# Expert block: 125-row transfers in two parts, the output bias ahead of the tiles, two gathers added in the next block, context roots moved

## What is computed

```python
# layer 0
q = _ln(latents, ...);  x = latents + _mha(q, q, ...)              # L0_sa
qc = _ln(x, ...);       kv = _ln(tokens, ...)
x = x + _mha(qc, kv, ...)                                          # L0_ca
h = _ln(x, ...);        logits = h @ rw.T + rb                     # L0_moe: 8 experts, 2 for each token
vals, idx = jax.lax.top_k(logits, K);  gates = softmax(vals)
h1 = gelu(einsum('nd,efd->enf', hf, fc1_w) + fc1_b[:, None, :])
eo = einsum('enf,edf->end', h1, fc2_w) + fc2_b[:, None, :]
x = x + (eo[idx_f, arange(N)[:, None], :] * gates_f[..., None]).sum(axis=1)
# layer 1
x = features + _mha(xn, xn, xn, ..., causal)                       # L1_sa
x = x + _mlp(_ln(x, ...), ...)                                     # L1_m1
x = x + _mha(_ln(x, ...), encoder_output, encoder_output, ...)     # L1_ca: keys and values of the raw context
x = x + _mlp(_ln(x, ...), ...)                                     # L1_m2
# layers 2 and 3: L2_ca, L2_m1, L2_sa, L2_m2, L3_ca, L3_m
```

## Time and profile before

| | us |
|---|---|
| median of 3 runs | 2048.26 |
| lowest, highest | 2045.43, 2050.31 |
| the profiled execution | 2057.58 |
| its span | 2055.8 |
| TensorE busy, weight loads busy | 1776.4, 1237.2 |
| DVE, ACT, POOL busy | 1332.9, 866.2, 629.1 |

### The profile page before, as it was taken

The page is one execution under the profiler, slowest core; times in us unless marked ns, Lnnn a source line. Parts: engine busy times, 40 slices in busy tenths (PEclk is TensorE's granted clock), DMA queues, the critical chain, the costliest instruction groups (busy, mean ns, idle before and its releaser), DMA issues.

```text
span 2055.8 us, 34270 instructions
## 1 busy us (share of the span) xinstructions
PE 1776.4 (86%) x10630; PEld 1237.2 (60%) x10630; DVE 1332.9 (65%) x3354; ACT 866.2 (42%) x2513; POOL 629.1 (31%) x732
## 2 busy tenths in 40 slices
PE   5969999769996878988779999896888979898988
PEld 4746665558985656655565555483444845455567
DVE  5866767301117876788666676796677966556665
ACT  3735554322334643565324444342332435444521
POOL 2325555210022234676320000130000325455534
PEclk9979998879998978999789999997998989999999
DMA  4100000468862000002100010101000100000200
GB/s 167 37 20 15 13 7 16 147 217 301 307 236 82 0 1 31 32 30 71 67 8 16 16 69 0 42 11 62 0 0 19 55 1 12 23 11 11 72 1 18
DMA packets 36627, 115.15 MB, mean 56 GB/s; under 512 B 2961, under 2 KB 23345, under 8 KB 29345
## 3 DMA queue, kind: packets, MB, share of 16 engines
q1 hardware_dynamic: 33968, 107.33, 15.2%
q0 software_dynamic: 2544, 6.43, 1.0%
HBM read 99.34 MB, written 14.40 MB: 55 GB/s over the span
## 4 chain that ended last, share of the span: by engine, by line
PE 44%; issue 20%; DVE 14%; POOL 14%; ACT 4%; DMA 3%; SPq 1%; POOLq 0%; DVEq 0%; ACTq 0%
POOL arena L2020 11%; PE ps L1008 7%; PE ps L1048 4%; PE ps L821 4%; PE ps L873 3%; PE ps L1168 3%; PE ps L1152 3%; PE ps L927 3%; PE ps L816 3%; PE ps L947 2%; PE ps L891 1%; PE ps L863 1%; DMA wml<-in_wm_L_moe 1%; PE ps L933 1%; ACT arena L1286 1%
## 5 line engine op out<-in xcount | busy, mean ns | idle before, releaser
L2020 POOL TENSOR_TENSOR arena<-arena,rinv 112x375 f32<-112x375 f32 (+1 forms) x448 | 371.1, 830 | 489.9 <-DVE rinv L1675 479.7
L891 PEld LDWEIGHTS ps<-cst,arena 112*125 112x125 f32 (+1 forms) x1408 | 188.1, 184 | 176.6 <-POOL arena L2020 88.9
L891 PE MATMUL ps<-cst,arena 112*125 112x112 f32 (+1 forms) x1408 | 247.0, 294 | 45.2 <-POOL arena L2020 39.9
L1286 ACT ACTIVATE arena<-ps,negmax 112x375 f32<-112x375 f32 (+1 forms) x384 | 190.6, 501 | 168.2 <-DVE negmax L1670 167.8
L1684 DVE COPY arena<-ps 125x336 f32<-125x336 f32 x384 | 190.8, 497 | 47.3 <-PE ps L891 44.9
L2073 POOL TENSOR_TENSOR w_split_sb<-wml,w_split_sb 128x512 fp32r<-128x512 f32 (+1 forms) x40 | 45.9, 1148 | 527.0 <-ACT w_split_sb L1352 525.1
L1670 DVE TENSOR_REDUCE negmax<-ps 112x1 f32<-112x375 f32 (+1 forms) x288 | 158.3, 550 | 70.9 <-PE ps L863 61.9
L1008 PE MATMUL ps<-h_split_sb,w_split_sb 128*128 128x448 f32 x768 | 179.7, 383 | 17.8 <-DVE h_split_sb L1559 7.1
L1286 ACT ACTIVATE arena<-arena,negmax 112x112 f32<-112x112 f32 (+1 forms) x256 | 125.4, 491 | 139.1 <-DVE negmax L1659 97.0
L1008 PEld LDWEIGHTS ps<-h_split_sb,w_split_sb 128*128 128x128 f32 x768 | 150.4, 198 | 35.9 <-DVE h_split_sb L1559 13.2
L816 PE MATMUL ps<-wat,arena 128*125 128x256 f32 (+1 forms) x608 | 153.5, 390 | 16.8 <-DVE arena L1600 9.5
(11 more groups left out here) (221 smaller groups left out, 3186.7 us busy)
## 6 DMA issues: line engine op xcount, KB each, us to landing
wml<-in_wm_L_moe SPq DMA_DIRECT2D x21, 1028.0 KB, 7.7
wml<-in_wm_L_moe SPq DMA_DIRECT2D x21, 1024.0 KB, 7.7
craw<-in_ctx SPq DMA_DIRECT2D x40, 375.0 KB
wml<-in_wm_L_m SPq DMA_DIRECT2D x3, 3072.0 KB, 13.8
wat<-in_wa_L_ca SPq DMA_DIRECT2D x2, 2560.0 KB, 10.2
wml<-in_wm_L_m SPq DMA_DIRECT2D x2, 2048.0 KB, 10.1
keys_hbm<-arena SPq DMA_DIRECT2D x8, 375.0 KB
values_hbm<-vz SPq DMA_DIRECT2D x8, 375.0 KB
```

Source lines behind the costliest of these rows:

```text
L891: last = nc.tensor.transpose(ps[0:blk.kp, T_BANK + s % blk.t_banks, o:o + S], buf[:, i * blk.nk + q * blk.kp:i * blk.nk + (q + 1) * blk.kp ...
L1286: last = go(probs[0:S, s % blk.nprobs, i * nk:(i + 1) * nk], src[:, i * nk:(i + 1) * nk], ACT.Exp, scale=-1.0 if blk.mask == "input" else ...
L2020: pool.tensor_tensor(p3, p3, r3, ALU.mult).then_inc(scaled, 1)
```

## The change

Five edits.

1. In the expert block each 125-row transfer (context loads, value stores) is issued as two: rows 0 to 111 and rows 112 to 124 (`transfer`). The semaphore counts follow (32 for each load, 48 for each pair of stores).
2. The output bias: the eight small matmuls stand together behind context 4 and ahead of tile 0, into banks 1 to 4; DVE adds all eight there, and TensorE waits for the eight adds before the up part of tile 0.
3. DVE adds the gathered rows of batches 0 to 5 at the end of the expert block and those of batches 6 and 7 at the end of batch 0 of L1_sa, with a second run of the 13 statistics operations for these two. `gate` gets a place of its own.
4. The context statistics of L0_sa: the means and variances (6 operations) and the roots for L0_ca (12) go into the drain of L0_sa, the roots for L3_ca (13) behind the last tile of the expert block.
5. `out_banks`: behind a dense feed-forward block batch 7 goes to bank 5, if the next block doesn't use bank 5 for its pieces (L1_m1, L2_m2 and L3_m).

```diff
+            def transfer(dst, src, signal):
+                for r in (slice(0, KP // 16 * 16), slice(KP // 16 * 16, KP)):
+                    sp.dma_start(dst[r], src[r]).then_inc(signal, 16)
...
-                    sp.dma_start(craw[:, m % 2], ctx[m + 2].rearrange("(k p) d -> p k d", p=KP)).then_inc(ahead_loaded[m % 2], 16)
+                    transfer(craw[:, m % 2], ctx[m + 2].rearrange("(k p) d -> p k d", p=KP), ahead_loaded[m % 2])
...
-                    sp.dma_start(values_hbm[m], v_ahead[:, m % 2]).then_inc(ahead_stored[m % 2], 16)
+                    transfer(values_hbm[m], v_ahead[:, m % 2], ahead_stored[m % 2])
...
-                    if 2 <= t < 2 + B:
-                        output_bias(t - 2, 4 + t % 2)
-                    elif 2 <= t - 2 < 2 + B:
-                        pe.wait_ge(bias_added, t - 3)
...
+                pe.wait_ge(b2_in, 16)
+                pe.wait_ge(gt_done, 1)
+                for b in range(B):
+                    mm(ps[0:S, 1 + b // 2, b % 2 * D:(b % 2 + 1) * D], gT[:, b * S:(b + 1) * S], b2_sb, start=True, stop=True).then_inc(out_full, 1)
                 pe.wait_ge(ahead_done, FIRST_AHEAD * NAHEAD)
                 turn_tile(0)
-                pe.wait_ge(gt_done, 1)
+                pe.wait_ge(bias_added, B)
                 tile_hidden(0)
...
+            def add_gathered(link, n, b):
+                dve.wait_ge(gathered[b], 16 * TOP)
+                link(v.scalar_tensor_tensor(X[:, b], results[b][:, 0], gate[:, 0, b:b + 1], X[:, b], ALU.mult, ALU.add))
+                v.scalar_tensor_tensor(X[:, b], results[b][:, 1], gate[:, 1, b:b + 1], X[:, b], ALU.mult, ALU.add).then_inc(out_done, 1)
+                dve.wait_ge(out_done, START[n]["out"] + b + 1)
+                take(b, X[:, b])
...
-                    if blk.reads_ctx and b == B - 1:
-                        dve.wait_ge(ctx_read, B)
-                        context_statistics(context)
-                        link = links[0] = Links(context.base + context.k)
...
+                        if blk.reads_ctx and b == B and s < blk.out_step:
+                            known = links[0].k
+                            if s == 0:
+                                dve.wait_ge(ctx_read, B)
+                            context_moments(links[0], s)
+                            if s == blk.out_step - 1:
+                                context_root(links[0], BLOCKS[n + 1])
+                            after[0] += links[0].k - known
...
+                    if b == 0 and behind_experts:
+                        last = Links(links[0].base + links[0].k)
+                        for b_ in range(2 * SOON, B):
+                            add_gathered(last, n - 1, b_)
+                        statistics(last, n, 2 * SOON, B)
+                        rest[0] = last.k
...
+                for later in BLOCKS[n:]:
+                    if isinstance(later, Attn) and later.norm_ctx:
+                        context_root(link, later)
+                add_gathered(link, n, 0)
+                statistics(link, n + 1, 0, 1)
...
+            return OUT_BANKS[:7] + ((1,) if n + 1 < len(BLOCKS) and 5 in BLOCKS[n + 1].w_banks else (5,))
```

108 lines of the change are left out of this document (52 added, 56 removed).

## The result

| | before | after |
|---|---|---|
| median of 4 runs each, one chip | 2049.28 us | 2019.69 us |
| their range | 2045.43 to 2052.42 | 2014.4 to 2023.9 |
| profiled execution, span | 2055.8 us | 2017.4 us |
| profiled execution, time | 2057.58 us | 2019.28 us |

The ratio of the runs is 0.9855 with a 95% interval of 0.9826 to 0.9884, so the change is worth 29.6 us; 34.7 were predicted, and the 2019.7 lies within the predicted 2000 to 2030. The two profiled spans differ by 38.4 us, 8.8 more than the medians.

What follows compares the result with a forecast made beforehand. TensorE is busiest, so time is gained where it waits (expert tiles' start, end of L0_sa, handover to L1_sa) or has less to do. Terms: -6.7 - 18.7 - 6.5 + 1 - 3.8 = -34.7 us, 2048.3 to 2014; range 2000 to 2030.

Steps and rivals of the forecast that it cites:

- The forecast's case: Whole kernel: all parts of the change together give 2014 us; 2000 to 2023 had a chance of 0.62.
- Context roots: L0_sa: 31 context statistics operations leave the front of batch 7, free in their new places; minus 6.7 us.
- Split transfers: Start of the expert tiles: weights of tile 2 land sooner, minus 16, and full clock, minus 2.7; taken minus 18.7 us.
- give the load 4 to 5 us: Load of tile 0's rows, issued at 413.91 as before; tile 0's up-projection then at 419.5 instead of 424.54.
- Bias: Expert tiles: eight tiles lose a bias matmul, minus 6.5 us; its new place ahead of tile 0 costs plus 1.
- Handover: Into L1_sa: first maximum 9.3 us sooner, moved adds cost 5.5 in the first batch; taken minus 3.8 us.
- Output banks: In front of L1_ca and L3_ca: batch 7's transposes no longer wait for DVE's second add; taken as 0.
- waits for DVE all the same: L1_ca and L3_ca: the next block's first transpose still waits for DVE, a little earlier; taken as 0.
- (1) Weights as the pace: Expert tiles: the queue gives only 290 GB/s, so weights set the pace; 2027 us, chance 0.16.
- (2) Two parts gain nothing: Split transfers: the two parts follow one another and landings stay as they are; 2035 us, chance 0.10.
- (3) SP's block counts transfers: Start of the expert tiles: SP's holds go by number of transfers, so more make it slower; 2052 us, chance 0.04.
- The sum: Whole kernel: minus 6.7, 18.7 and 6.5, plus 1, minus 3.8, in all minus 34.7 us, from 2048.3 to 2014.

Runs made afterwards that it cites:

- one_transfer: The changed kernel with each 125-row load and store of the expert block as one transfer again: 2033.17 us, ratio 0.9917 to the kernel before.
- split_115_10: The changed kernel with the 125 rows cut as 115 and 10 instead of 112 and 13: 2032.8 us; the changed kernel on that chip 2014.68.
- two_parts_alone: The kernel before with only the split of the 125-row transfers into 112 and 13 rows: 2034.97 us, ratio 0.9894 to the kernel before.
- late_weights: The changed kernel with three weight requests (3 MB) issued behind the last early context's stores: 2017.35 us; the changed kernel on that chip 2020.84.
- banks_alone: The kernel before with only the new output banks: 2047.3 us, ratio 0.9983 to the kernel before.
- old_banks: The changed kernel with the old output banks: 2022.53 us; the changed kernel on that chip 2014.68.

## Why the prediction was right, and where it was not

The forecast's case came true, and 2014 was 5.7 us too low. By its own steps:

**Context roots:** minus 6.7 was forecast, with a range to minus 7.5. Measured, 6.8: the lag of before is 0.9 us ahead of batch 7 and 7.7 at its maximum. Less the 0.9 it is 7.0 at the update of the drain, 6.1 in L0_ca and 7.5 at the gates; undoing the part gives 6.7 at the maximum and 7.5 to 8.1 behind it. The drain had less slack than it seemed (0.16 us of idle left), but TensorE, not the roots, still ended last there.

**Split transfers:** minus 16 and minus 2.7 were forecast. The mechanism is shown: one_transfer brings the holds back, and split_115_10 shows that what counts is the cut at a multiple of 16 rows. The size was off. Tile 2 started 20.5 us sooner; less the 8.5 that stood at the gates, that is 12.1, and 2.6 from the clock: 14.7 instead of 18.7. The step that failed is "give the load 4 to 5 us", after the scatters had been left as they were. Counted from the gates, the row loads were issued 1.0 us later than before, since the last scatter took 7.02 us to land, and the load took 6.53 (6.8 in two_parts_alone), both behind weights that the faster contexts let SP issue sooner. So tile 0 came 1.4 us sooner against the gates instead of 5.0. two_parts_alone shows it bare, with 7.71 us of waiting for rows, and late_weights shows the cause: without 3 MB ahead of them the rows are there in time. Two smaller things nearly cancel: tile 0 ran in part at half clock and took 5.21 us instead of 3.81, which no step had, and tile 2 didn't wait the 2 us for its weights that were allowed for. Context 4 was to end 7.8 us behind the start of the gates; it took 8.1 and 8.6 us in two traces and 10.4 in the first, where its keys ran at half clock. It didn't matter, since the rows came later still.

**Bias:** minus 6.5 for the period is exact (8.05 to 7.24 and 7.25 us). Its new place was put at plus 1 and costs 0 to 0.5, since the wait for the rows covers it. That cover is itself the miss of the step before: in late_weights the bias is what stands in front of tile 0.

**Handover:** minus 9.3 in front and plus 5.5 behind were forecast, together minus 3.8. Against the trace of before it is minus 8.9 and plus 6.4, minus 2.5. But against banks_alone, whose code is before's up to there, it is minus 6.9 and plus 9.2, which is a loss of 2.3. So the runs do not show that this step gained anything. The cause was assigned wrongly too. The sum took all of the 9.3 for the adds and none for the split. The runs show that the split alone brings the first maximum forward by 2.3 to 4.3 us, and the moved adds by 4.6 more at a price of 5.8 to 6.3. Moving them is a loss of 1 to 2 us in this kernel.

**Output banks:** 0 was forecast. The step "waits for DVE all the same" is right for TensorE's first transpose and overlooks SP, which asks for the next block's keys and values when the output transposes are done. That is worth 1.5 us at the first scores of L1_ca; L3_ca was not read.

**The rivals.** (1) Weights as the pace: no up-projection waits for weights, and the period is 7.24 to 7.25; the expert slices moved up to 327 GB/s, and this rival held 326 to be too much. (2) Two parts gain nothing: fell for the cut at 112, true for the one at 115. (3) SP's block counts transfers: fell; it is held 10.19 us with one transfer and 0.34 with two, at the same key store.

**The sum** by the traces up to the third batch of L1_sa is minus 8.5, minus 14.7, minus 6.6 with the new place of the bias, minus 2.5: minus 32.3, of which 0.9 stood there before the change begins. The same sum against banks_alone is minus 25.2. The medians differ by 29.6 us, between the two. Behind that point the two spans part by 6 us more in L1_ca, 1.5 for the banks and 4.5 in the stretch at half clock, which no step had. Against the medians the traces of before and of the changed kernel show 8.8 us too much, and 8.3 of it is that the profiled execution of before was that much over its median. So the parts are known from these traces to some microseconds and not better, and that the total came out only 5 us from the forecast is in part luck: a split worth 4 us less and a handover whose gain isn't shown stand against roots, banks and bias that gave some 3 us more.

## What to carry to other kernels

Look at the number of rows of a transfer before its size: 125 rows held up the queue and SP behind it, 112 and 13 didn't, and 115 and 10 did again. When such a load gets faster, ask what SP will now issue sooner and whose small transfer stands behind it; here it was the 128 KB of rows that TensorE needed first. And work that is moved from ahead of a stage into it is only free if its engine has idle time there: the moved adds saved 4.6 us in front of L1_sa and cost 5.8 to 6.3 inside it. Last, before a part is called worth 2 us, look at two traces of the same code: here they were 5.7 us apart at 760 us.

## What the runs showed of the hardware

- SP's issue of one transfer takes 0.34 us when the queue is free and was held up to 10.19 us by 125-row transfers in flight; with the large part at 112 rows no issue of the changed kernel took over 1.21 us from 384 to 432 us, at DMA shares of 0.97 to 1.05 from 392 to 416 us. In late_weights the 13-row part of a value store was held 2.75 us.
- The loads of 128 KB of rows took 6.5 to 6.8 us with some 3 MB of weights requested ahead of them (changed kernel, two_parts_alone), and at most 4.5 us with these requests behind them (late_weights).
- The granted clock after two waits of some 3 us stayed at 1.2 GHz for 10.2 to 23.9 us in the same piece of L1_ca, the same for one kernel in three traces, and different between kernels that reach it half a microsecond apart. It stayed there though TensorE was busy for whole stretches of 4 us, as the rows of old_banks show.
- In late_weights TensorE had no idle from 399.94 us to the end of the bias at 410.1, and still ran at 0.50 from 408 us on; tile 0 then took 6.76 us instead of the 3.81 in the earlier trace rows. Of the 3.0 us by which tile 0 started sooner 1.5 were left at tile 1.
